# A graph network on one core: the relational phases multiply near rows by all eight relations at once and pick one by the type's bits

## The reference, cut to what matters

```python
def rgcn_conv(x, src, dst, edge_type, W, root, bias):      # x: 3125 x 16, W: 8 x 16 x 16
    x_src = x[src]
    msg = jnp.zeros((src.shape[0], W.shape[2]), x.dtype)
    for r in range(NUM_RELATIONS):
        msg = msg + jnp.where((edge_type == r)[:, None], x_src @ W[r], jnp.zeros((), x.dtype))
    cnt = jnp.zeros((num_nodes, NUM_RELATIONS), x.dtype).at[dst, edge_type].add(1.0)
    norm = 1.0 / jnp.maximum(cnt[dst, edge_type], 1.0)
    agg = jax.ops.segment_sum(msg * norm[:, None], dst, num_segments=num_nodes)
    return agg + x @ root + bias
```

## Time and profile before

| what | value |
|---|---|
| runs | 4555.11 us median of 3 (4553.6 to 4555.17) |
| profiled execution | 4555.6 us |
| its span, first to last instruction | 4553.4 us |
| mean granted TensorE clock | 0.983 |
| busy shares of the span | PE 95%, PEld 72%, DVE 91%, ACT 71%, POOL 72% |
| chain that ended last, by engine | PE 81%, DVE 10%, issue 5%, ACT 2%, DMA 1%, SPq 1% |

### The profile page before, as it was taken

One profiled execution on the slowest core, in us unless ns is written; L12 is line 12 of the kernel. 1 busy time (PEld: TensorE's weight loads), 2 busy tenths in 40 slices (PEclk: granted clock), 3 DMA queues, 4 the chain that ended last, 5 costly groups with the idle time before them and its releaser, 6 DMA issues.

```text
span 4553.4 us, 107759 instructions
## 1 busy us (share of the span) xinstructions
PE 4339.6 (95%) x30477; PEld 3261.8 (72%) x30477; DVE 4121.4 (91%) x11864; ACT 3235.6 (71%) x5359; POOL 3284.9 (72%) x2515
## 2 busy tenths in 40 slices
PE   4999999999997999999979999998999999799998
PEld 3777777777775777777747777776777777566665
DVE  5999999999997999999969999997999998888887
ACT  3777777777774777777737777775777777677776
POOL 4888888888883777777727777775777775688886
PEclk8999999999998999999989999999999999899999
DMA  3111111111111222222211111111111111111111
GB/s 72 21 17 18 17 18 17 18 18 18 18 17 40 61 59 61 59 60 60 59 37 27 27 28 27 27 28 39 27 28 28 26 28 23 30 31 31 30 31 24
DMA packets 336556, 148.67 MB, mean 33 GB/s; under 512 B 250040, under 2 KB 322532, under 8 KB 336392
## 3 DMA queue, kind: packets, MB, share of 16 engines
q0 software_dynamic: 104000, 59.31, 10.1%
q1 hardware_dynamic: 232517, 88.88, 7.8%
HBM read 135.45 MB, written 9.80 MB: 32 GB/s over the span
## 4 chain that ended last, share of the span: by engine, by line
PE 81%; DVE 10%; issue 5%; ACT 2%; DMA 1%; SPq 1%; DVEq 0%; POOL 0%; POOLq 0%; ACTq 0%
PE acc L600 37%; PE rows_ps L757 16%; PE rows_ps L693 7%; PE bank L773 5%; PE bank L693 4%; PE counts L607 3%; PE eaT_ps L765 3%; DVE raw L1258 2%; PE rows_ps L681 2%; DVE stationary L1234 2%; PE eaT_ps L669 1%; DVE one_hot L1206 1%; PE counts L604 1%; DVE rows_ps L1321 1%; ACT stack L928 1%
## 5 line engine op out<-in xcount | busy, mean ns | idle before, releaser
L600 PE MATMUL acc<-one_hot,stationary 125*128 125x392 bf16 x12000 | 2335.4, 329 | 39.5 <-DVE stationary L1234 35.1
L584 POOL DMA_INDIRECT gathered<-table_l,row_numbers x1200 | 1607.3, 1339 | 461.1 <-issue 349.1
L600 PEld LDWEIGHTS acc<-one_hot,stationary 125*128 125x128 bf16 x12000 | 1157.3, 100 | 709.0 <-DVE stationary L1234 49.9
L866 ACT ACTIVATE distances<-count_hi,fields 125x392 bf16<-125x392 f16 (+1 forms) x2500 | 1227.5, 560 | 0.0
L1234 DVE TENSOR_TENSOR stationary<-mask,parts 125x1024 bf16<-125x1024 bf16 x1500 | 943.3, 683 | 0.3 <-ACT mask L851 0.2
L851 ACT CAST mask<-is_lo 125x1024 bf16<-125x1024 f32 x500 | 523.1, 1046 | 447.3 <-DVE is_lo L1187 393.5
L584 POOL DMA_INDIRECT fields_all<-table_l,row_numbers x500 | 646.3, 1293 | 259.6 <-issue 114.8
L1206 DVE TENSOR_SCALAR one_hot<-count_hi,fields 125x392 bf16<-125x392 f16 x2300 | 734.4, 341 | 13.5 <-issue 13.5
L1321 DVE COPY_PREDICATED rows_ps<-near_bits_now,rows_ps 125x320 f32<-125x320 int8 (+3 forms) x1600 | 579.7, 362 | 162.6 <-PE rows_ps L757 118.6
L584 POOL DMA_INDIRECT gathered<-table_l2a,row_numbers x400 | 512.7, 1282 | 282.6 <-DVE parts L1216 119.4
L757 PE MATMUL rows_ps<-node_parts,h1T 125*125 125x192 bf16 (+1 forms) x7200 | 678.3, 252 | 27.0 <-DVE node_parts L1285 19.6
(11 more groups left out here) (213 smaller groups left out, 4706.6 us busy)
## 6 DMA issues: line engine op xcount, KB each, us to landing
near_key<-near_keys_by_chunk SPq DMA_DIRECT2D x300, 122.1 KB
gathered<-table_l,row_numbers POOLq DMA_INDIRECT x1200, 2.8
fields<-edge_fields SPq DMA_DIRECT2D x500, 31.2 KB
near_key<-near_keys_by_chunk SPq DMA_DIRECT2D x100, 91.6 KB
fields_all<-table_l,row_numbers POOLq DMA_INDIRECT x500, 3.5
gathered<-table_l2a,row_numbers POOLq DMA_INDIRECT x400
gathered<-table_l2b,row_numbers POOLq DMA_INDIRECT x400
ea<-in_edge_attr SPq DMA_DIRECT2D x100, 62.5 KB
```

Of the source, the lines that this page charges most:

```text
L584: pool.indirect_dma_start(out=gathered[ph][:, s, t, :], in_=table[ph], out_offset=None, in_offset=bass.IndirectOffsetOnAxis(ap=row_numbers ...
L600: mm = pe.matmul(acc[:, :], stationary[:, s, k, t, :, :].rearrange("p a b -> p (a b)"), one_hot[:, s, t, :], start=first and t == 0 and k ...
L866: ins = act.activation(distances[:, i * n:(i + 1) * n], count_hi[:, 0:n], ACT.Abs, scale=-1.0, bias=fields[:, s, k, t:t + 1].bitcast(F32))
```

## The change

- Near rows of l2a and l2b are no longer multiplied with the type's one-hot. ACT copies the four picked rows side by side (64 columns) into `near_outer` (`near_gather`), PE transposes them once, and one matmul with the first 64 rows and 512 columns of the block-diagonal `bd["rel1"]` or `bd["rel2"]` gives the messages of all eight relations for the four tiles.
- The type's three bits, made once at the start on DVE and copied for each chunk by ACT (`near_types_of`), choose one of eight by three predicated copies within the message bank (`pick`).
- The body `l2` gets the picks at its head, its one-hots move between them, and ACT's order gets the two new copies.
- `near_types`, `near_type`, `near_is_type` and `relations` with its two DMAs go. l1 keeps its computation.

```diff
-        near_type = sb("near_type", [EP, CHUNKS, NEARS])
+        near_type_bits = sb("near_type_bits", [EP, CHUNKS, NEARS], I32)
+        near_types_now = sb("near_types_now", [EP, 2, NEARS], I32)
...
-            "l2a": ("is_lo", "msg", "hi", "rest", "mid", "low"),
+            "l2a": ("is_lo", "four", "two", "one", "msg", "hi", "rest", "mid", "low"),
...
             def near_turn(ph, chunk, s):
                 pe.wait_ge(near_outers, chunks_before(ph) + chunk + 1)
+                if ph != "l1":
+                    pe.transpose(turned_ps[:, 0:EP], near_outer[:, 0:128], ident[0:EP, 0:EP]).then_inc(near_turned, 1)
+                    return
...
             def near_messages(ph, chunk, s):
                 pe.wait_ge(near_copied, chunks_before(ph) + chunk + 1)
-                weights = message_weights[:, :] if ph == "l1" else relations[:, "ab".index(ph[2]), :]
+                if ph != "l1":
+                    n = NEAR_OF[ph][s]
+                    pe.matmul(bank[MESSAGE_BANK[s]][0:EP, 0:n * W], near_outerT[0:n * F, 0:EP],
+                              bd["rel" + str("ab".index(ph[2]) + 1)][0:n * F, 0:n].rearrange("p a r f -> p (a r f)"),
+                              start=True, stop=True).then_inc(near_done, 1)
+                    return
...
-                act.copy(near_outerT[:, 0:NEAR_OF[ph][s] * EP], turned_ps[:, 0:NEAR_OF[ph][s] * EP]).then_inc(near_copied, 1)
+                rows, n = (128, NEAR_OF[ph][s] * EP) if ph == "l1" else (NEAR_OF[ph][s] * F, EP)
+                act.copy(near_outerT[0:rows, 0:n], turned_ps[0:rows, 0:n]).then_inc(near_copied, 1)
...
+            def near_gather(ph, chunk, s):
+
+                act.wait_ge(near_picked, chunks_before(ph) + chunk + 1)
+                act.wait_ge(near_turned, chunks_before(ph) + chunk)
+                n = NEAR_OF[ph][s]
+                act.copy(near_outer[:, 0:n * F].rearrange("p (t f) -> p t f", f=F),
+                         near_rows_ps[ph][:, 0:n, 0, :]).then_inc(near_outers, 1)
+
+            def near_types_of(ph, chunk, s):
+
+                if later(chunk, 2):
+                    act.wait_ge(S[ph]["step"], done(ph, "one", chunk - 2))
+                n = NEAR_OF[ph][s]
+                types = near_type_bits[:, bass.ds(chunk, 1), NEARS - n:].rearrange("p c k -> p (c k)")
+                act.copy(near_types_now[:, s, 0:n].bitcast(I8), types.bitcast(I8))
...
                 def body(chunk, pair, s):
+                    if relational:
+                        near_types_of(ph, chunk, s)
                     masks(ph, chunk, s)
-                    hi_distances(ph, chunk, pair, s, end=ph == "l2a" or ph == "l2b")
+                    hi_distances(ph, chunk, pair, s, end=False)
+                    if relational:
+                        if later(chunk, 1) and follows(chunk, 1):
+                            near_gather(ph, chunk + 1, 1 - s)
+                        hi_distances(ph, chunk, pair, s, begin=False)
                     if later(chunk, 1) and follows(chunk, 1):
-                        near_result(chunk + 1, 1 - s)
+                        near_result(chunk + 1, 1 - s, gather=False)
...
+            near_types = typ[:].rearrange("p (c t) -> p c t", t=T)[:, :, T - NEARS:]
+            link(dve.scalar_tensor_tensor(near_work[2][:, :, 0:NEARS], near_types, 7, near_types, ALU.logical_shift_left, ALU.bitwise_or))
+            dve.wait_ge(ev("near_bits_made"), 1)
+            link(dve.scalar_tensor_tensor(near_work[1][:, :, 0:NEARS], near_work[2][:, :, 0:NEARS], 14, near_work[2][:, :, 0:NEARS],
+                                          ALU.logical_shift_left, ALU.bitwise_or))
+            link(dve.tensor_tensor(near_type_bits[:], near_work[1][:, :, 0:NEARS], bit_of_byte[:, 2:3, None].to_broadcast([EP, CHUNKS, NEARS]),
+                                   ALU.bitwise_and))
...
                 halve(2).then_inc(near_halved, 1)
-                if ph == "l2a" or ph == "l2b":
-                    near_types(ph, chunk, s)
...
-                if ph == "l3":
+                if ph != "l1":
                     return
...
                 def l2(chunk, pair, s):
                     st = Steps(ph, chunk, s)
                     slot_free(ph, chunk)
+                    n = far(ph, s)
+                    by_type = bank[MESSAGE_BANK[s]][0:EP, 0:(T - n) * W].rearrange("p (t r f) -> p t r f", r=RELATIONS, f=F)
+                    bits = near_types_now[:, s, 0:T - n].bitcast(I8).rearrange("p (k b) -> p k b", b=4)
+
+                    def pick(bit):
+
+                        dve.sem_inc(near_begun, 1)
+                        chosen = bits[:, :, bit:bit + 1][:, :, :, None].to_broadcast([EP, T - n, 1 << bit, F])
+                        st.mark(dve.copy_predicated(by_type[:, :, 0:1 << bit, :], chosen, by_type[:, :, 1 << bit:2 << bit, :]))
+
+                    dve.wait_ge(near_done, chunks_before(ph) + chunk + 1)
+
+                    dve.wait_ge(masked, before(ph) + chunk + 1)
+                    pick(2)
                     one_hots(ph, s, (0,))
-                    n = far(ph, s)
-                    dve.wait_ge(near_done, chunks_before(ph) + chunk + 1)
-                    dve.tensor_tensor(msg[:, s, n:T, :], bank[MESSAGE_BANK[s]][0:EP, 0:(T - n) * F].rearrange("p (t f) -> p t f", f=F),
+                    st.wait("four")
+                    pick(1)
+                    one_hots(ph, s, (1,))
+                    st.wait("two")
+                    pick(0)
+                    one_hots(ph, s, (2,))
+                    st.wait("one")
+                    dve.tensor_tensor(msg[:, s, n:T, :], by_type[:, :, 0, :],
...
-                    one_hots(ph, s, (1,))
                     st.wait("msg")
-                    split(st, msg[:, s], lambda k: one_hots(ph, s, ((2, 3), (4, 5), (6, 7), ())[k]))
+                    split(st, msg[:, s], lambda k: one_hots(ph, s, ((3,), (4, 5), (6, 7), ())[k]))
```

More of the change, by code:

```diff
@@ L503, in stream_l0 @@
                         if chunk == 2:
-                            for i in range(2):
-                                sp.dma_start(relations[:, i, :],
-                                             A[f"L2_gnn_W{i + 1}"].rearrange("r i o -> (r i) o")).then_inc(ev("diagonals_in"), 16)
                             sp.dma_start(message_weights[:],
@@ L743, in _ @@
             turn_h("l1")
-            pe.wait_ge(ev("diagonals_in"), 16 * (8 * LO + 4))
+            pe.wait_ge(ev("diagonals_in"), 16 * (8 * LO + 2))
             wide("l1", "msg")
@@ L994, in masks_and_near, with near_result @@
             def masks_and_near(ph):
-                def near_result(chunk, s):
+                relational = ph == "l2a" or ph == "l2b"
+                def near_result(chunk, s, gather=True):
                     if ph == "l3":
@@ L998, in near_result @@
                     else:
+                        if relational and gather:
+                            near_gather(ph, chunk, s)
                         near_copy(ph, chunk, s)
@@ L1179, in _ @@
             dve.wait_ge(ev("fields_converted"), FIELDS - 1)
-            dve.tensor_copy(near_type[:], fields_all[:, :, TYPE, T - NEARS:T].bitcast(F32))
             def scalar_field(s, k, t):
@@ L1285, in split_nodes @@
                 link(dve.tensor_tensor(part[2], left, part[1], ALU.subtract), event)
-            def near_types(ph, chunk, s):
-                n = NEAR_OF[ph][s]
-                number = near_type[:, bass.ds(chunk, 1), :].rearrange("p c j -> p (c j)")
-                number = number[:, number.shape[1] - n:]
-                dve.tensor_tensor(near_is_type[:, 0:n], count_key[:, None, 0:LO].to_broadcast([EP, n, LO]),
-                                  number[:, :, None].to_broadcast([EP, n, LO]), ALU.is_equal)
             def near_begin(ph, chunk, pair, s, groups=(0, 1)):
@@ L1343, in near_finish @@
                 where(0, rows[:, :, 0:1, :], rows[:, :, 1:2, :]).then_inc(near_picked, 1)
-                if ph == "l3":
+                if ph != "l1":
                     return
                 dve.wait_ge(near_picked, before_this + 1)
-                if later(chunk, 1) or ph != "l1":
+                if later(chunk, 1):
                     dve.wait_ge(near_turned, before_this)
-                if ph == "l1":
-                    dve.tensor_copy(near_inverse[:, s, 0:count], rows[:, :, 0, F:ROW1])
-                    factor = near_ea8[:, bass.ds(chunk, 1), :].rearrange("p c (t r) -> p (c t) r", t=NEAR1)[:, NEAR1 - count:]
-                else:
-                    factor = near_is_type[:, 0:count]
-                dve.tensor_tensor(near_outer[:, 0:count], rows[:, :, 0:1, 0:F].to_broadcast([EP, count, RELATIONS, F]),
+                dve.tensor_copy(near_inverse[:, s, 0:count], rows[:, :, 0, F:ROW1])
+                factor = near_ea8[:, bass.ds(chunk, 1), :].rearrange("p c (t r) -> p (c t) r", t=NEAR1)[:, NEAR1 - count:]
```

(1 more changed line is left out.)

8 lines of the change are left out of this document (3 added, 5 removed).

## The result

The changed kernel took 4637.31 us, the median of 4 runs from 4634.98 to 4639.71, against 4554.35 for the kernel before (4553.06 to 4555.17): a ratio of 1.0182 with the interval 1.0165 to 1.02. It is slower by 83 us, where 12 us of gain were forecast, and lies outside the range of 4504 to 4574.

What follows compares the result with a forecast made beforehand. PE bounds the kernel before at 7.26 us a chunk; DVE was to take over at 7.21. 4555.6 - 9.7 (194 chunks at 0.05) - 3.8 + 1.6 = 4543.7, given as 4543 us, range 4504 to 4574.

Steps and rivals of the forecast that it cites:

- DVE's sum: DVE's chunk in l2a and l2b: 6.85 us plus 0.36 for the picks gives 7.21, above PE's 7.02.
- The three waits ahead of `pick(2)`: At DVE's head, three waits and an increment, unpriced by any row: between nothing and 0.14 us, the middle taken.
- PE's part: PE's chunk in l2a and l2b: 7.26 - 0.32 for transposes + 0.08 for the message matmul = 7.02 us.
- That it uses 64 rows of the array instead of 128 changes nothing in the columns that pass: PE's message matmul of 512 columns costs 0.86 us despite half the rows, 0.08 more than before.
- rival 1: PE still sets the pace: unpriced waits hide, fills no longer collide, PE's 7.02 us counts; 4506 us, chance 0.18.
- `where(0)` to `pick(2)`: 0.40: DVE's head of a chunk: 0.33 us mean start distance with the loop end, plus the waits' middle, gives 0.40.
- The loop end: At DVE's head, every second chunk idles another 0.29 us after `where(0)`, making 0.52 instead of 0.14.
- rival 3: Moved one-hots on DVE collide with POOL's gathers: three add 0.15 us, chunk 7.36, 4572 us; chance 0.20.
- My argument against it: DVE's one-hots and fills together take 2.17 us in l2a and 2.16 in l3, as if collisions were limited.
- Rival 4: Each moved one-hot is held in full by POOL's lock: 0.66 us more, DVE's chunk 7.87, 4671 us; chance 0.03.
- The sign that the prediction named: The forecast is wrong if DVE's fills and one-hots change their means by more than 50 ns together.
- Outside the loop: Integer operations at the start add 1.6 us; shorter near paths at both relational phases' starts save 3.8 us.

Runs made afterwards that it cites:

- quiet_after: The changed kernel without POOL's gathers in l2a and l2b, zeros in place of the far rows: 4566.25 us, ratio 1.0028 to the kernel before.
- nopick: The changed kernel without its three predicated picks, their counts raised by plain semaphore increments: 4565.99 us, ratio 1.0026.
- rotate: The changed kernel with DVE's loop turned, so that a pass ends behind the long stationary products: 4604.18 us, ratio 1.0109.
- rot_128: The changed kernel with DVE's loop turned and the message matmul over all 128 rows: 4603.55 us, ratio 1.011.
- rot_hoist_128: The changed kernel with DVE's loop turned, the picks' waits put ahead of `where(0)`, and a 128-row message matmul: 4527.56 us, ratio 0.9951.
- late: The changed kernel with DVE's four one-hots moved from between the picks to behind hi, rest and mid: 4637.89 us, ratio 1.0187.
- quiet_before: The kernel before the change without POOL's gathers in l2a and l2b, zeros in place of the far rows: 4552.40 us, ratio 1.0.
- best_low: The changed kernel with turned loop, moved waits, 128 rows, five one-hot tiles on ACT, and gathers waiting for low, not msg: 4548.17 us, ratio 0.999.

## Why the prediction was wrong

Two terms of DVE's sum were too small, so it came to 7.21 us where 7.69 was measured. The moved one-hots were counted as if no gather could lengthen them: 0.28 us a chunk. The three waits ahead of `pick(2)` were counted at 0.07 and took 0.24. A step in PE's part failed too, but it did not set this kernel's time.

**PE's part, wrong in one step.** One transpose at 0.11 was right. "That it uses 64 rows of the array instead of 128 changes nothing in the columns that pass" failed. The slot was 1.05 and not 0.86, and the next 12 sums took 0.10 more; PE's chunk was 7.30 and not 7.02. Shown by `quiet_after` and `nopick`, and by the 24 us that 128 rows gave back. Why a 64-row matmul holds up two weight loads stays open. In the kernel after this is hidden behind DVE; it turns rival 1, with its 4506, into a floor near 4566 that no relief of DVE gets under.

**DVE's head, where the waits were too cheap.** That DVE becomes the bound, that its wait for `rows_ps` goes and that it idles at the head of every second body was right. "`where(0)` to `pick(2)`: 0.40" was 0.59. The loop end was priced nearly right: 0.52 - 0.14 = 0.38 in every second body, and it took 0.80 - 0.38 = 0.42. The waits were not: I took 0.07 and allowed 0.14 at most, "between nothing and 0.14", and the body without a loop end took 0.38 where l3 shows 0.14, so they cost 0.24. `rotate` shows the first (33 us back from moving the loop end), `rot_128` against `rot_hoist_128` the second.

**The collisions, rival 3 with twice its size.** My sum had this term at nothing. Rival 3 allowed 0.15 us a chunk for three one-hots that move under the gathers, at a chance of 0.20; measured were 0.28 over four. `quiet_after` shows that the gathers make it, `late` that the position does. My argument against it, that one-hots and fills together take the same in both phases, was wrong: the fills kept their 448 ns and the one-hots added theirs. Rival 4, each held in full, would have cost 0.66 a chunk; what was measured lies between the two. The sign that the prediction named for this came: the two means changed by 69 - 8 = 61 ns together, more than 50.

With the head and the one-hots put right the sum of DVE's chunk comes to 7.68, as worked out above, and 194 chunks at 0.42 more than before to 81 us, less the savings outside the loop. l2a and l2b grew by 76.3.

**Outside the loop, nearly right.** The first gather starts at 38.58 us and not 36.59, so the integer operations cost 2.0 us where 1.6 was forecast. The first sums begin 1.9 us sooner after the start of l2a and 2.6 after that of l2b, 4.5 together where 3.8 was forecast. All ahead of l2a came out 0.8 us shorter even so; what made up for the 2.0 is open, and kernels from the one after reach l2a anywhere between 2344.3 and 2359.9. At the start of l2a the first pick waits 2.10 us for ACT's mask, which I had called ready more than a microsecond before; in the steady chunks no such wait shows.

**l3, not foreseen.** Every kernel made from the one after has 697.7 to 700.2 us behind l2b, with or without its gathers or picks in l2, against 690.7 in the kernel before and 690.3 in `quiet_before`. Timeline of DVE in l3 after, the head of a pass and of the second body (compare):

```profile
4282.12 0.50 DVE L1351 COPY_PREDICATED rows_ps<-near_bits_now,rows_ps 125x320 f32<-125x320 int8 x1 [0.47 <-PE rows_ps L753]
...
4284.35 0.97 DVE L1243 TENSOR_SCALAR one_hot<-count_hi,fields 125x392 bf16<-125x392 f16 x2 [0.17 <-issue]
...
4295.16 0.50 DVE L1351 COPY_PREDICATED rows_ps<-near_bits_now,rows_ps 125x320 f32<-125x320 int8 x1 [0.45 <-PE rows_ps L753]
```

Two chunks take 4295.16 - 4282.12 = 13.04 us, where they took 12.86 before (4203.48 to 4216.34). The loop end costs 0.17 there and not 0.29, but the fills take 409 ns instead of 352 and the one-hots 381 instead of 365: the same instructions take longer. That they fall differently beside POOL's gathers, as in l2a, is likely but not shown, and what moved them is open; no experiment changed l3 alone.

**The whole.** Of the 96 us between forecast and profile (11.9 of gain forecast, 84.3 of loss), 90 lie in l2a and l2b (76.3 of loss, and 13.5 of gain forecast there), 9 in l3, and the start gives 2 back.

## What to carry to other kernels

When a change moves work from one engine to another that is only a few per cent less busy, price the new head of the chain with its waits and the loop end, put the waits where the engine stands still anyway, and look for a long instruction to put the loop end behind: here the same work in another order was worth 2.3% (1.0182 to 0.9951, with the full rows), and the moved waits were the largest single part. Give a matmul among full-row ones all its rows, with zeros, rather than half of them. And before a gain is claimed for an engine that is relieved, measure that engine's own chunk with the other one taken away: two kernels, one without gathers and one without picks, showed a floor of 7.30 us under which no further work on DVE could help.

## What the runs showed of the hardware

- A matmul of 64 rows between others of 125 and 128 rows did not get its weights ahead, and neither did the next one: 0.32 and 0.76 us of idle time of the loader, 1.05 us for 512 columns in two records instead of 0.86, and 0.10 more for the 12 behind it.
- A `tensor_scalar` on DVE and a gather that POOL issues lengthen each other where the first crosses the end of the second: up to 0.70 instead of 0.32 us for a one-hot, 0.72 instead of 0.34 for a fill, and 1.75 and more (at most 2.38, in `late`) instead of 1.21 for the gather. Inside a gather they keep their time. Not every crossing costs both: 82 one-hots crossed an end in the kernel before at 0.314 us, and in `late` POOL alone pays. A one-hot during which a gather begins took 0.37. Moving one group out of the way put another in it, in `late` (POOL pays) and in `best_low` (the one-hots pay).
- An end of a loop pass behind short dependent instructions cost DVE 0.80 - 0.38 = 0.42 us. Behind 1.9 us of products it cost at most 0.10 (0.48 against 0.38 in `rotate`).
- Three waits for semaphores that the profile shows as already raised, and an increment, cost DVE 0.38 - 0.14 = 0.24 us ahead of an instruction that does not depend on the one before. Put where DVE waits for its own result anyway, they cost next to nothing (0.14 and 0.22 from start to start).
